# Two attention stages reordered: a 16-head attention loop written out with its input rows prepared one pair ahead, and 8-head local-attention layers with their mask added on VectorE

## The reference, cut to what matters

```python
# third block: 16 heads of 16 columns, causal
def _L1_attn_ref(x, Wqkv, Wo):
    ...
    q = cos * q + rotate_half(q) * sin
    k = cos * k + rotate_half(k) * sin
    scores = jnp.einsum('bhqd,bhkd->bhqk', q, k) / math.sqrt(DH)
    scores = jnp.where(causal, scores, -jnp.inf)
    attn = jax.nn.softmax(scores, axis=-1)
    out = jnp.einsum('bhqk,bhkd->bhqd', attn, v)
    ...
    return out @ Wo.T
# fourth block: two layers, 8 heads of 64 columns, windows of 128 rows
def _layer(x, wqkv, qs, ksc, wo, lg, lb, w1, b1, w2, b2):
    h = shift_token(x)
    q, k, v = jnp.split(h @ wqkv, 3, axis=-1)
    ...
    o = local_attention(q, k, v)     # each window sees itself and the one before it
    x = x + o @ wo
    h = shift_token(x)
    h = (h - mu) / jnp.sqrt(var + 1e-05) * lg + lb
    a, g = jnp.split(h @ w1 + b1, 2, axis=-1)
    return x + (a * jax.nn.gelu(g, approximate=False)) @ w2 + b2
...
x = x + _L0_attn_ref(_layernorm(x), ...)
x = x + _L0_ffn_ref(_layernorm(x), ...)
x = x + _L1_attn_ref(_layernorm(x), ...)
x = x + _L1_ffn_ref(_layernorm(x), ...)
```

## Time and profile before

| What | us |
| --- | --- |
| Median of 3 runs | 3048.98 |
| Lowest and highest of the 3 | 3030.15 and 3049.12 |
| The profiled execution, its own time | 3019.5 |
| Its span, first to last instruction | 3017.8 |
| Span in `phase_attn1`, one trip (first L1042 to the next) | 749.87 to 919.26: 169.4 |
| Span in `phase_layer`, one pair (L1615 of the second pair to that of the third) | 1640.25 to 1831.85: 191.6 |

### The profile page before, as it was taken

The page is one execution under the profiler, slowest core; times in us unless marked ns, Lnnn a source line. Parts: engine busy times, 40 slices in busy tenths (PEclk is TensorE's granted clock), DMA queues, the critical chain, the costliest instruction groups (busy, mean ns, idle before and its releaser), DMA issues. The chain is left out here.

```text
span 3017.8 us, 49703 instructions
## 1 busy us (share of the span) xinstructions
PE 2436.8 (81%) x18074; PEld 1856.3 (62%) x18074; DVE 1850.3 (61%) x3821; ACT 1227.9 (41%) x3259; POOL 1026.3 (34%) x1332
## 2 busy tenths in 40 slices
PE   7888187885887878685789888898877888988988
PEld 4555187774544455453667667676666676766766
DVE  4555287876747566574755656557556575575745
ACT  1111043432453625353543634536326245363362
POOL 1111432323434333242552514325126153252431
PEclk9988599998787888888899999999988999989999
DMA  3222510012001010111100000000020000000000
GB/s 104 74 74 73 209 31 28 24 31 85 22 3 57 3 43 17 43 16 64 59 16 15 2 15 15 16 15 2 1 107 2 29 15 23 22 1 29 15 2 28
DMA packets 81364, 107.58 MB, mean 36 GB/s; under 512 B 6972, under 2 KB 72720, under 8 KB 80656
## 3 DMA queue, kind: packets, MB, share of 16 engines
q1 hardware_dynamic: 76192, 93.12, 9.2%
q0 software_dynamic: 3456, 9.44, 1.2%
q10 hardware_dynamic: 1520, 2.31, 0.2%
HBM read 65.66 MB, written 38.67 MB: 35 GB/s over the span
## 5 line engine op out<-in xcount | busy, mean ns | idle before, releaser
L1549 POOL TENSOR_SCALAR l_probs<-l_probs,l_rinv 128x256 f32<-128x256 f32 (+1 forms) x512 | 222.2, 454 | 206.1 <-DVE l_rinv L1635 206.1
L1028 DVE TENSOR_REDUCE c_cnmax<-cbank 128x1 f32<-128x384 f32 (+3 forms) x384 | 205.4, 594 | 100.0 <-PE cbank L1208 98.2
L1802 ACT ACTIVATE l_probs<-l_bank,l_nmax 128x256 f32<-128x256 f32 (+1 forms) x512 | 222.6, 449 | 80.0 <-DVE l_nmax L1631 79.6
L1533 POOL TENSOR_TENSOR l_work<-l_work 128x512 f32<-128x512 f32 x64 | 82.7, 1293 | 458.6 <-DVE l_work L1617 457.7
L1120 ACT ACTIVATE c_cprobsT<-cbank 128x384 f32<-128x384 f32 (+1 forms) x384 | 180.5, 522 | 95.6 <-PE cbank L1234 95.0
L1919 PE MATMUL l_bank<-l_kT,l_flipped 64*128 64x256 f32 (+1 forms) x1024 | 178.0, 410 | 28.8 <-ACT l_probs L1802 28.8
L1962 PE MATMUL l_bank<-l_flipped,l_v 128*64 128x128 f32 x1792 | 126.6, 279 | 82.2 <-ACT l_oT L1817 53.3
L577 POOL TENSOR_TENSOR m_w_low<-w,m_w_high 128x1024 fp32r<-128x1024 f32 x39 | 106.0, 2719 | 241.5 <-DVE m_w_high L597 241.5
L1631 DVE TENSOR_REDUCE l_nmax<-l_bank 128x2 f32<-128x512 f32 (+1 forms) x256 | 147.6, 616 | 35.5 <-PE l_bank L1926 33.9
L1962 PEld LDWEIGHTS l_bank<-l_flipped,l_v 128*64 128x64 f32 x1792 | 98.3, 137 | 108.7 <-ACT l_flipped L1812 91.5
L1658 DVE COPY l_flipped<-l_turned 128x256 f32<-128x256 f32 (+1 forms) x256 | 88.1, 385 | 123.3 <-PE l_turned L1946 122.2
(11 more groups left out here) (256 smaller groups left out, 6973.1 us busy)
## 6 DMA issues: line engine op xcount, KB each, us to landing
w<-in_W1T SPq DMA_DIRECT2D x8, 1024.0 KB, 6.6
w<-in_W2T SPq DMA_DIRECT2D x8, 1024.0 KB, 10.8
l_came<-y_d SPq DMA_DIRECT2D x16, 512.0 KB, 3.9
a_came<-in_X SPq DMA_DIRECT2D x10, 512.0 KB, 5.5
xs_d<-zrow SPq DMA_DIRECT2D x8, 640.0 KB, 9.8
c_came<-x_d SPq DMA_DIRECT2D x10, 512.0 KB, 3.8
m_xs<-xs_d SPq DMA_DIRECT2D x39, 128.0 KB, 2.1
ys_d<-m_y SPq DMA_DIRECT2D x39, 128.0 KB, 1.7
```

The lines of the kernel that those rows point to most:

```text
L1028: dve.tensor_reduce(nmax[:, c % 2, qt, s, i:i + n], S, AX, ALU.max, negate=True).then_inc(nmax_ready[s], 1)
L1549: pool.tensor_scalar(probs[s][:, u % 3, h, 0:n], probs[s][:, u % 3, h, 0:n], rinv[s][:, u, h:h + 1], 1.0, ALU.mult, ALU.mult)\
L1802: act.activation(probs[s][:, u % 3, h, 0:n], bank[s][u % 2][:, 2 * P * h:2 * P * h + n], ACT.Exp, bias=nmax[s][:, u, h:h + 1], accum_out=r ...
```

## The change

**`phase_attn1`.** The hardware loop becomes a Python loop inside one block: the four pairs are written out, without a barrier between them, and all semaphore counts grow with the pair. `x` now alternates between two buffers (`rows_of`), into which the gather writes directly; the normalised rows are written over `came`. The start of the next pair is moved: DVE does it (`first_norm(pair + 1)`) after the last row maximum and before the division, GpSimd's power lies within its unit loop, and PE turns the next pair's rows behind each stream's product with Wo. PE turns both streams' outputs first and multiplies then. The two casts of high parts go from DVE to ACT (`high_parts`). The four small DMAs that primed two semaphores go, with the waits on them.

**`phase_layer`.** The two mask matmuls go. DVE instead adds the mask and takes the extremum in one instruction for each head, which writes masked negated scores into `probs`; ACT takes the exponential from there, in place, with scale -1. The bank of the scores is free once DVE has read it, not once ACT has. The turned probabilities and the outputs of both streams are copied out by one instruction. The lags grow from 2 and 3 to 3 and 4 units, PE's order in a step becomes turn, scores, output, and the product with wo is spread over the last steps. Both shifts stand together behind it. Three activation tables are loaded ahead by instructions of their own.

```diff
         def gather(pool, s, pair):
             for t in range(NT):
-                pool.indirect_dma_start(yrow[s][:, t, :], None, g.ys_d,
+                pool.indirect_dma_start(rows_of[pair % 2][s][:, t, :], None, g.ys_d,
...
-        with nc.Fori(0, PAIRS) as pair:
-            with nc.Block() as block:
+        with nc.Block() as block:
...
+                    def first_norm(trip):
+                        rows = rows_of[trip % 2]
+                        for s in range(NS):
+                            if trip:
+                                dve.wait_ge(x_in[s], trip * 16)
+                            dve.wait_ge(y_in[s], trip * (16 * NT) + 16 * NT)
+                            dve.tensor_tensor(rows[s][:], came[s][:], rows[s][:], ALU.add).then_inc(x2_ready[s], 1)
+                            dve.wait_ge(x2_ready[s], trip + 1)
+                            row_stats(dve, chain, var_ready[s], lambda t: [rows[s][:, t, :]], stats[s], mv[s], ve[s])
+                        for s in range(NS):
+                            for ins in normalised_rows(dve, rstd_ready[s], trip + 1, lambda t: [rows[s][:, t, :]], mv[s], rstd[s],
+                                                       lambda t: [xn[s][:, t, :]]):
+                                ins.then_inc(xn_ready[s], 1)
...
-                        twice = [P, H1, 2, DH1]
-                        hi = [(qhl[s][:, :, 0::3, :], q), (khl[s][:, :, 0:2, :], k)]
-                        for dst, src in hi:
-                            dve.tensor_copy(dst, src.unsqueeze(2).to_broadcast(twice)).then_inc(high_ready[s], 1)
...
+                        for dst, src in [(qhl[s][:, :, 0::3, :], q), (khl[s][:, :, 0:2, :], k)]:
+                            act.activation(dst, src.unsqueeze(2).to_broadcast([P, H1, 2, DH1]), ACT.Copy).then_inc(high_ready[s], 1)
...
                     for u in range(UNITS):
                         for s in range(NS):
                             row_max(s, u)
+                    if pair + 1 < PAIRS:
+                        first_norm(pair + 1)
                     for k in range(2 * NT):
                         outputs(k)
...
-                        pe.wait_ge(oT_ready[s], DC)
+                    for s in range(NS):
+                        pe.wait_ge(oT_ready[s], pair * DC + DC)
...
+                        if pair + 1 < PAIRS:
+                            transposes(s, pair + 1)
-            nc.all_engine_barrier(sems_to_clear=sem_range)
+        nc.all_engine_barrier(sems_to_clear=sem_range)
...
                     def row_max(s, u):
-                        w = units[s][u][1]
+                        n = 1 + min(units[s][u][1], 1)
+                        if u == 1:
+                            dve.wait_ge(qkT_psum[s], pair * (2 * NT) + 2 * NT)
                         dve.wait_ge(scores_ready[s], pair * UNITS + u + 1)
-                        S = bank[s][u % 2][:].rearrange("p (h k) -> p h k", h=2)
-                        dve.tensor_reduce(nmax[s][:, u, :], S[:, :, 0:(1 + min(w, 1)) * P], AX, ALU.max, negate=True).then_inc(nmax_ready[s], 1)
+                        if u >= 3:
+                            dve.wait_ge(pT_psum, pair * UNITS + u - 2)
+                        ban = g.mask[:, 3 - n:3, :].rearrange("p a b -> p (a b)")
+                        for h in range(2):
+                            dve.tensor_tensor_reduce(probs[s][:, held(u), h, 0:n * P], bank[s][u % 2][:, 2 * P * h:2 * P * h + n * P], ban, -1.0, 3e38,
+                                                     ALU.add, ALU.min, nmax[s][:, u, h:h + 1]).then_inc(nmax_ready[s], 1)
...
+                        if i == len(turns):
+                            act.preload_act_table(ACT.Exp)
...
                             if u >= 2:
-                                pe.wait_ge(probs_ready[s], pair * (2 * UNITS) + 2 * (u - 1))
+                                pe.wait_ge(nmax_ready[s], pair * (2 * UNITS) + 2 * (u - 1))
...
-                            for part in range(2):
-                                for s in streams:
-                                    cp, w, half = units[s][u]
-                                    n = 2 if w else 1
-                                    r = slice(DH2 * half, DH2 * (half + 1))
-                                    last = pe.matmul(bank[s][u % 2][:, 2 * P * h:2 * P * h + n * P], g.mask[r, 3 * part, :],
...
-                    for u in range(UNITS + 3):
+                    for u in range(UNITS + OUT_LAG):
+                        if 0 <= u - FLIP_LAG < UNITS:
+                            flip(u - FLIP_LAG)
                         if 2 <= u < UNITS:
                             scores(u)
-                        if u >= 3:
-                            output(u - 3)
-                        if 2 <= u < UNITS + 2:
-                            flip(u - 2)
...
+                        if u >= OUT_LAG:
+                            output(u - OUT_LAG)
+                        if u == UNITS:
+                            pe.wait_ge(late_in, LATE_ALL)
+                        for s in range(NS):
+                            if u >= UNITS:
+                                attended(s, u - UNITS)
...
-                    for t in range(NT):
-                        attended(0, t)
-                    attended(1, 0)
                     shift(0)
-                    for t in range(1, NT):
-                        attended(1, t)
+                    shift(1)
                     flip_hn(0)
-                    shift(1)
```

411 lines of the change are left out of this document (209 added, 202 removed).

## The result

The changed kernel takes 2914.65 us (median of 4 runs, 2906.51 to 2915.02), the kernel before 3048.75 in the same session (3030.15 to 3049.12). The ratio is 0.957, with a 95% interval of 0.953 to 0.961. The forecast of 2960 had the sign and stood 45 us high; the result lies 0.35 us under the low end of its range, 2915.

What follows compares the result with a forecast made beforehand. Loose places were taken to be handoffs, at pair boundaries and in the layers' loop head and tail. From 3019.5 us, 46 for attention and 40 for layers left 2933.5, scaled to 2962, predicted 2960; range 2915 to 3010.

Steps and rivals of the forecast that it cites:

- Attention, boundaries: Between pairs of `phase_attn1`: next pair's start hidden in VectorE's idle stretch, 15.3 us gained at each of three, 46 us.
- Attention, turns: Turns in `phase_attn1`: 0 us, since TensorE is full there; bounds -1 and +3.5 us a pair.
- D: Rival: ScalarE sets the 16-head attention's turns, 4.6 instead of 4.2 us each, costing 14 us; 2976 us, chance 0.08.
- Layers: `phase_layer`: quicker loop head, unit loop and tail, less what is given back; 5 us a pair, 8 pairs, 40 us.
- The serial stretch: Layers, end of product with wo to first feed-forward matmul: 11.5 us with TensorE nearly idle, where it was 4.5.
- The clock term: Start of the layers' feed-forward part: first matmuls may run at 1.2 instead of 2.4 GHz, 1.1 us lost.
- rival C: Layers' loop runs at its engines' sums, unit 2.75 us, clock stays up: 9 us a pair; 2928 us, chance 0.12.
- First pairs of a layer: Unit loop where GpSimd also splits weights: the longer lag was to cover that as well as before.
- Price of the fused instruction: VectorE in the layers' unit loop: 0.47 us a head with its read; from 0.68 the change would be slower.
- Rival A: Layers gain nothing: the loop's 8 us is given back in statistics, norm and clock; 3003 us, chance 0.20.
- The scaling: Whole kernel: sum of 2933.5 us scaled by 1.0098, before's median over its profiled execution, to 2962.
- The add beside GpSimd: `phase_attn1`: moved add beside GpSimd's zeroing could be held up about 2.4 us a pair; left out of the sum.

Runs made afterwards that it cites:

- attn_only: The kernel before with the changed `phase_attn1` alone, `phase_layer` as it was: 2965.99 us, ratio 0.981 to before.
- tail: Changed kernel with three quarters of the second stream's product with wo put back behind the first stream's shift: 2866.31 us, ratio 0.949 to before.
- late_low: Changed kernel with GpSimd's weight-splitting subtractions moved behind the unit loop of each layer's first pair: 2896.29 us, ratio 0.959 to before.

## Why the prediction came out as it did

- **Attention, boundaries: right.** 46 us predicted, and the three boundaries give 14.8 + 16.0 + 16.0 = 46.8. The gap on TensorE is gone, VectorE's second norm is what is left, and the cover held.
- **Attention, turns: mis-sized; that the stage's sum fits is in part luck.** Rotary products of later turns lie 3.7 us apart where they lay 4.1, and from the first to the last of a pair it takes 23.7 us (24.9 in the first pair) instead of 27.2: some 13 us over four pairs, where I had taken 0 with a bound of 1 a pair because TensorE was "full". It speaks against D. In the explained profile all of it is lost again behind the turns. 1.8 us a pair go where the prediction feared it: the first row maximum comes 12.3 us after the last rotary product, before 10.5. Most of the rest lies in the units (first row maximum to last), which take 73.5 to 73.9 us in three of its pairs and 70.8 to 71.8 in `attn_only`, where the stage gains 53.8 us and not 46.4.
- **Start of the stage: missed.** I counted 0 for the priming DMAs, since the gather ends later. The first add came at 746.35 instead of 749.87. I did not test which wait it was.
- **Layers: mechanism right, size too small.** 40 us predicted, 54.7 found. For the second pair: scores of unit 4 come 13.5 us behind those of unit 0 instead of 19.5, 6.0 earlier and not 3.5. From there to unit 15 it takes 30.6 us, predicted 31.4, before 36.1. From there to the end of the product 23.8 us, predicted 23.2. The serial stretch has 11.3, predicted 11.5. In all the feed-forward part starts 9.9 us earlier (0.7 of it from the turns), not 6.1. The largest miss is the head of the loop.
- **The clock term was not there.** The first feed-forward matmuls do run at 0.50, but the stretch from the first of them to the next pair has 61.7 us as before (61.8), and in `tail`, where they run at full clock, 61.6, so the 1.1 us was a loss without an effect on the end. A later pair so gains 8.8 us, rival C's 9, but not in C's way: C wanted a serial stretch of 8 us or less and a unit of 2.75 us (11 x 2.75 - 1.6 = 28.7 us from unit 4 to unit 15; found 30.6), and what came instead is the shorter head.
- **First pairs of a layer: wrong.** "Its longer lag covers that as well as before" failed: these two gain 1.9 and 0 us as a whole (up to the feed-forward part 2.4 and 3.3; behind it the second had 63.8 us before, and 68.2 in `attn_only` with the same code). A third unit of lag doesn't cover 6 us of one instruction on GpSimd, whose scalings are then late for the turns. `late_low` shows it. Without this miss the layers would have gained 54.7 + 15.1 = 69.8 us, near C's 72.
- **Price of the fused instruction: too high, and so the threshold.** 0.345 us, not 0.47. Twice that costs 66 us of the layers, and leaves 39 of the 105. From there on VectorE is full, so each further 0.1 us a head would cost, by the prediction's formula, 8 x 13 x 4 x 0.1 = 42 us (the loop has 12 wide units, not 13: 38 us); the turning point then is an estimated 0.76 or 0.77 us a head, not 0.68.
- **Rival A: half of it true.** The serial stretch gives back 6.8 us a pair, 54 us, which is as much as the layers gain net. `tail` gets 40 of them back.
- **The scaling: wrong.** I multiplied by 1.0098, because before's median stood that far over its profiled execution. In the three later sessions before's medians were 3020.95, 3038.07 and 3024.70, near or above the profiled 3019.5, and the changed kernel's own profile is its median. The factor belonged to those executions, as far as these few show, and did not carry over. It added 29 us; the terms above make 19 more, and rounding 2962 to 2960 took 2 off: 45 us in all.

**The add beside GpSimd.** The contention that the prediction named shows here, though on another instruction. GpSimd's cast of the row maxima (L952) takes 0.20 us in seven of the eight places of a pair, and in the eighth, here at the first boundary, where the moved add runs from 870.04 to 871.25, it takes until that add is over:

```profile
861.27 0.20 POOL L952 CAST c_nmax_hl<-c_cnmax 128x16 fp32r<-128x16 f32 x1 [0.39 <-DVE c_cnmax L1040]
...
870.25 1.06 POOL L952 CAST c_nmax_hl<-c_cnmax 128x16 fp32r<-128x16 f32 x1 [0.40 <-DVE c_cnmax L1040]
```

So it is at all three boundaries (1.06, 1.06, 1.07), and at none before the change. The add has its 1.21 to 1.23 us as at the start of the stage, where nothing lies beside it. The Trainium skill, "SBUF — State Buffer", section "Who interferes with whom", has a VectorE instruction with two inputs in SBUF contend with a GpSimd instruction that reads SBUF; the trace agrees, with GpSimd the one that waits, 0.86 us a pair instead of the 2.4 that I had worked out for the zeroing. The zeroing beside the second add takes 0.96 us for two, where two take 0.78 to 0.89 elsewhere, so it is hardly touched.

## What to carry to other kernels

A lag and the order within a step are one decision: put the oldest work first only if it is old enough, or the loop becomes one chain. When work is spread into the last steps of a loop, ask what it used to cover; keep for the serial stretch behind it as much work of the other stream as that stretch is long. Add up a gain from one profile as a difference: the ratio of median to profile of the kernel before said nothing of the kernel after. And where the same code varies by 5 to 10 us from one profile to the next, take the price of an edit from the shortest stretch that holds it.

## What the chip showed that I had not expected

- A fused VectorE instruction and the read of its accumulator cost 0.34 to 0.35 us for 256 elements, less than the 0.42 us that its row shows: a following one starts before it ends, and the read is hidden.
- Lag 2 instead of 3, with nothing else changed, took a later pair's loop from 44.9 to 91.1 us and the median from 2914.65 to 3287.36 us, more than any gain in this study.
- The same 10 us of the untouched `phase_attn0` ran at a granted clock of 0.50 in one execution and of 0.67 in another, and four steps of 3 to 4 us of this kind moved the start of `phase_attn1` by 14 us.
